# Vision tower block with routed experts: the residual travels halved with each fetched row

## The chip, the cores and the metric

The kernel runs on one core of a Trainium2 chip. The core has five engines that run their own instruction streams and meet only at semaphores: TensorE (PE, matmul; its weight loads are listed as PEld), VectorE (DVE), ScalarE (ACT), GpSimd (POOL) and SyncE (SP, which here only issues transfers). Sixteen DMA engines move data between HBM and the on-chip memory (SBUF). The metric is the device time of one execution in microseconds (us); less is better.

## The reference, cut to what matters

```python
h = tok(x, W)                                  # 64 images x 36 patches, 192 channels: 2304 tokens
h = h + attn(layernorm(h), W_attn, b_attn, W_o, b_o)      # 12 heads, causal
flat = layernorm(h).reshape(-1, 192)
probs = softmax(flat @ router_w.T)             # 8 experts
top_w, top_i = top_k(probs, 2); top_w = top_w / top_w.sum(-1)
out = 0
for e in range(8):
    w_e = sum(top_w * (top_i == e))
    out = out + w_e * (gelu(flat @ w1[e] + b1[e]) @ w2[e] + b2[e])   # 192 -> 768 -> 192
return h + out                                 # layernorm: (x - mean) / sqrt(var + 1e-5)
```

## The kernel before

Tokens are worked on in 22 tiles (`NT`) of 108 rows (`TT`, three images); the last tile has only 36 real rows (`LAST`). Every product is made of fp16 high and low parts, three matmuls for one.

**Embedding and attention.** `embed` and `h_out` (ACT) fill `H`, the residual of all 22 tiles side by side in SBUF (108 x 22*192 fp32). A software pipeline over steps `i` then runs attention for tile `i`, and `residual(i - 2)` (DVE, L694) adds the projected output to `H`. `stats2` and the norm2 functions make the second layer norm of the tile from `H`; its high and low halves go to the row buffer `RB` (in `REG`), 194 fp32 words a token: 192 words of normed data (`rows2`) and two words `GAP` and `SECOND` for the gate weights.

**Routing.** After the last tile DVE chooses two experts for each token, and counts, ranks and places the 4608 (token, expert) pairs in a table of 43 tiles (`NS`) of 128 rows, each tile of one expert. `SOURCE` says which token each of the 128 rows of a tile reads, `TARGET` to which row of `yrows` its result goes (spare rows past the end for empty places). Meanwhile SP, once the gates are made (`route` at `GATES`) and the normed rows are done (`n2_lo`), stores `RB` to `xrows` in HBM in one transfer (L363).

**Experts.** For each of the 43 tiles `s`: POOL gathers 128 rows of `xrows` into a ring of four buffers `XR` (`gather_rows`, L435); PE transposes them (`transpose_rows`, L1107); DVE copies the transposes to `YT` and makes the gate of each row (`rows_out`, L870 and L873); PE multiplies by W1 (`up`, L1140); ACT does gelu and its fp16 high half (`hidden`, L596 and L601), DVE the low half (`hidden_lo`, L610); PE multiplies by W2 (`down`, L1156, the bias at L1161); DVE scales the PSUM result by the gate into `YO` (`gated`, L885); POOL scatters `YO` to `yrows` (`store_rows`, L440). Order by hand: POOL issues gathers 0 to 5, then for each `s` store `s` and gather `s + 6`. PE's iteration `s` holds `up(s + 2)`, `transpose_rows(s + 4)`, `down(s)`. A gather waits until its ring buffer was transposed (`xr_mm`) and its gate read (`gate_done`).

**Last pass.** The two results of a token lie side by side in `yrows`. In five batches (`BATCHES`, of 6, 6, 6, 3 and 1 token tiles) SP loads both parts (L368), DVE adds the first part to `H` and then the second (L907), and SP stores the batch to `out` (L371). All five loads are issued before the first store, on the one queue of SP.

Of the kernel before, what the change touches and what calls it, by code (L numbers as in the profile page):

```python
# [26 lines left out]
TT = TI * T  # L27
# [16 lines left out]
TOPK = 2  # L44
ST_ = 128
NS = TOPK * B * T // ST_ + E - 1
GAP, SECOND, ROW = C, C + 1, C + 2
SPARE = NS * ST_
CODED = 2048 // TT
CODES = 2 * TOPK  # L50
# [1 line left out]
S_X, S_W = 2.0 ** 8, 2.0 ** 10  # L52
S_XW = S_X * S_W
S_Q, S_V, S_P, S_G = 2.0 ** 6, 2.0 ** 8, 2.0 ** 12, 2.0 ** 6
EPS = 1e-5
PRODUCTS = [(0, 0), (0, 1), (1, 0)]
LAST_COLUMN = 2 * 127
LOADED = 8
# [8 lines left out]
def build(nc, xt, wtok, wqkv, wo, wr, w1, w2, idf, idh, selq, causal, kmask, eid,  # L67
# [3 lines left out]
    with ctx:  # L71
# [30 lines left out]
        WSTG = sb("WSTG", [128, WSLOTS * F])  # L102

        XW = KT * TT
        REG = sb("REG", [128, max(6 * XW, NT * ROW)])
        XHL = REG[:, 4 * XW:6 * XW].bitcast(F16)
        XS = [REG[:, n * XW:(n + 1) * XW] for n in range(4)]
        XS += [W1R[1][:, 2 * (E * F - n * XW):2 * (E * F - (n - 1) * XW)].bitcast(F32) for n in range(XSLOTS - 4, 0, -1)]
        RB = REG[0:TT, 0:NT * ROW]
        RBH = RB.bitcast(F16)  # L110

        KROW = 2 * 2 * 2 * TT
# [35 lines left out]
        G = PTR[:, 0:2 * F]  # L148
        GP = [PTR[:, (2 + p) * F:(3 + p) * F].bitcast(F16) for p in range(2)]

        XRS = 4
        XR = [REG[:, 6 * 2 * C + n * ROW:6 * 2 * C + (n + 1) * ROW] for n in range(XRS)]

        BATCHES, at = [], 0
        for tiles, home in ((6, REG[0:TT, 0:6 * 2 * C]), (6, W2[0][0:TT, 0:6 * 4 * C].bitcast(F32)),
# [112 lines left out]
            return buf[:, t % 2 * cols:(t % 2 + 1) * cols]  # L268

        def rows2(t, at, cols):  # L270
            return RBH[:, t * 2 * ROW + at:t * 2 * ROW + at + cols]

        PIECES = 2 * E
        PROJ, ROUT = 208, 448
# [9 lines left out]
            return range(max(0, 3 * i // 2), min(2 * PIECES, 3 * (i + 1) // 2))  # L284

        FIRST_NORM, GROUP, DRAIN = 8, 4, 3
        EMBEDDED = {11: -6, 13: -5, 15: -4, 17: -3, 19: -2, 21: -1}

        def has(t):
# [23 lines left out]
        @block.sync  # L313
        def _(sp):
            def patches(t):
                sp.dma_start(XS[t % XSLOTS], xt[t]).then_inc(x_in[t % XSLOTS], 16)

            def values_in(t):
                need(sp, vl_done, t + 2)
                need(sp, o_mm, t - 2)  # L320
                ring = t % VRING
                for b in range(TI):
                    for h in range(GH):
                        src = VP[b * T:(b + 1) * T, :].rearrange("p (t h r) -> p t h r", t=VRING, h=GH)[:, ring:ring + 2, h, :]
                        dst = VB[h * T:(h + 1) * T, :].rearrange("p (t b h r) -> p t b h r", t=VRING, b=TI, h=GH)[:, ring:ring + 2, b, h, :]
                        sp.dma_start(dst, src).then_inc(v_in[t // 2 % 2], 16)

            def weights(n):
                need(sp, w_lo, n - WSLOTS + 1)
                slot = n % WSLOTS * F  # L330
                at = n % PIECES
                if n < PIECES:
                    sp.dma_start(WSTG[0:HCP, slot:slot + F], w1[:, at * F:(at + 1) * F]).then_inc(w_in[n % WSLOTS], 16)
                else:
                    half = W2E // 2
                    sp.dma_start(WSTG[:, slot:slot + half], w2[:, at * half:(at + 1) * half]).then_inc(w_in[n % WSLOTS], 16)

            sp.dma_start(LANDED[0], wtok).then_inc(raw_in[0], 16)
            for t in range(XSLOTS):
                patches(t)  # L340
            for n in range(1, len(SMALL)):
                sp.dma_start(LANDED[n], SMALL[n][0]).then_inc(raw_in[n], 16)
            for dst, src in CONSTS:
                sp.dma_start(dst[:, :], src).then_inc(const_in, 16)
            for t in range(XSLOTS, NT):
                sp.wait_ge(xl_done, t - XSLOTS + 1)
                patches(t)
            for n in range(WSLOTS):
                weights(n)
            sp.wait_ge(consts_set, FILLS)  # L350
            for i in range(-2, NT + 1):
                for n in pieces(i - 1):
                    if n + WSLOTS < 2 * PIECES:
                        weights(n + WSLOTS)
                if has(i + 2) and i % 2 == 0:
                    values_in(i + 2)

            sp.wait_ge(s_mm, NT)
            for dst, src in LATER:
                sp.dma_start(dst, src).then_inc(later_in, 16)  # L360
            sp.wait_ge(n2_lo, NT)
            sp.wait_ge(route, GATES)
            sp.dma_start(xrows.rearrange("(t p) c -> p t c", p=TT), RB.rearrange("p (t c) -> p t c", c=ROW)).then_inc(rows_stored, 16)  # L363
            for u in range(2):
                sp.wait_ge(y_stored[u], 16 * ((NS + 1 - u) // 2))
            for n, (t, tiles, home) in enumerate(BATCHES):
                rows = yrows[t * TT * TOPK:(t + tiles) * TT * TOPK, :].rearrange("(t p k) c -> p t (k c)", t=tiles, k=TOPK)
                sp.dma_start(home.rearrange("p (t c) -> p t c", t=tiles), rows[0:home.shape[0]]).then_inc(parts_in[n], 16)  # L368
            for n, (t, tiles, home) in enumerate(BATCHES):
                sp.wait_ge(summed, 2 * n + 2)  # L370
                sp.dma_start(out[t * TT:min((t + tiles) * TT, B * T), :].rearrange("(t p) c -> p t c", t=tiles),  # L371
                             H[0:home.shape[0], t * C:(t + tiles) * C].rearrange("p (t c) -> p t c", c=C)).then_inc(out_stored, 16)
            sp.wait_ge(out_stored, 16 * len(BATCHES))
# [3 lines left out]
        def _(gp):  # L377
# [53 lines left out]

            def gather_rows(s):
                need(gp, xr_mm, s - XRS + 1)
                need(gp, gate_done, s - XRS + 1)
                gp.indirect_dma_start(out=XR[s % XRS], out_offset=None, in_=xrows,  # L435
                                      in_offset=bass.IndirectOffsetOnAxis(ap=SOURCE[:, s:s + 1], axis=0)).then_inc(rows_in[s % XRS], 16)

# [2 lines left out]
                gp.indirect_dma_start(out=yrows, out_offset=bass.IndirectOffsetOnAxis(ap=TARGET[:, s:s + 1], axis=0),  # L440
                                      in_=YO[s % 2], in_offset=None).then_inc(y_stored[s % 2], 16)

            gp.wait_ge(rows_stored, 16)
            gp.wait_ge(table, 5)
            for s in range(6):
                gather_rows(s)
# [8 lines left out]
        def _(act):  # L455
# [8 lines left out]

            def h_out(t):
                act.wait_ge(emb_mm, t + 1)
                nc.scalar.activation(htile(t), bank(5 + t % 2, TT, C), ACT.Copy, scale=1 / S_XW).then_inc(h_done, 1)

            def inverse_deviation(n):
                a, b = NORMS[n]  # L470
# [137 lines left out]
        def _(dve):  # L608
# [82 lines left out]
            def residual(t):  # L691
                need(dve, op_mm, t + 1)
                need(dve, o_mm, upto(t + 2))
                nc.vector.scalar_tensor_tensor(htile(t), bank(6, TT, 512)[:, PROJ:PROJ + C], 1 / S_XW, htile(t), ALU.mult, ALU.add).then_inc(h2_done, 1)  # L694

            def logits(t):
                need(dve, r_mm, t + 1)
# [92 lines left out]
            last = CHOSEN[:, (NT - 1) * E:NT * E]  # L790
            nc.vector.tensor_scalar(last, last, REAL[:, 0:1], None, ALU.mult).then_inc(route, 1)

            carry = RB.rearrange("p (t c) -> p t c", c=ROW)
            dve.wait_ge(gap_exp, 1)
            nc.vector.tensor_scalar(col[6], col[1], 1.0, S_G * S_W, ALU.add, ALU.mult).then_inc(route, 1)
            routed(15)
# [84 lines left out]
            def gated(s):  # L881
                dve.wait_ge(down_mm, s + 1)
                dve.wait_ge(gate_done, s + 1)
                need(dve, y_stored[s % 2], 16 * (s // 2))
                nc.vector.tensor_scalar(YO[s % 2], bank(4 + s % 2, ST_, C), GATE[:, s:s + 1], None, ALU.mult).then_inc(y_done, 1)  # L885

            rows_out(0)
            rows_out(1)
# [11 lines left out]
            for n, (t, tiles, home) in enumerate(BATCHES):  # L900
                dve.wait_ge(parts_in[n], 16)
                part = home.rearrange("p (t k c) -> p t k c", t=tiles, k=TOPK)
                for k in range(TOPK):
                    if k:
                        dve.wait_ge(summed, 2 * n + 1)
                    h = H[0:home.shape[0], t * C:(t + tiles) * C].rearrange("p (t c) -> p t c", c=C)
                    nc.vector.tensor_tensor(h, h, part[:, :, k, :], ALU.add).then_inc(summed, 1)  # L907


        @block.tensor  # L910
# [352 lines left out]
```

## Time and profile before

| | |
|---|---|
| median of 3 runs | 481.61 us (478.01 to 483.15) |
| the profiled execution | 475.52 us, of it the span from first to last instruction 473.6 us |
| PE busy | 372.1 us (79%) |
| DVE busy | 276.4 us (58%) |
| ACT busy | 221.1 us (47%) |
| POOL busy | 189.3 us (40%) |
| mean granted TensorE clock | 0.889 |

The profile is of one execution. Its stages, in us from the start of the span: embedding and attention up to about 230, routing 230 to 259, experts 259 to 450, last pass 452 to 473. Busy shares are averages over these stages, so each is looked at by itself: what a wait in one of them is worth is read from its timeline.

### The profile page before, as it was taken

To read this page: it belongs to the slowest core of one execution; us is meant where nothing else is said; L and a number is where in the kernel's file an instruction comes from. 1 tells how busy PE (TensorE), PEld (TensorE's weight loads), DVE (VectorE), ACT (ScalarE), POOL (GpSimd) and SP (SyncE) were. 2 spreads that over 40 slices of the span, in tenths; PEclk is the share of its full clock that TensorE was granted. 3 is DMA by queue.
4 is the path that set the end of the run, shared out by engine and by line. 5 is a ranking of instruction groups with operands and counts; after the bars stand their busy time and mean duration, and the time that the engine had idled before them with its cause. 6 is when DMAs were issued, how large, how long until landed. Compare 5 with 4: busy or idle time off the path is not lost.

```text
span 473.6 us, 16224 instructions
## 1 busy us (share of the span) xinstructions
PE 372.1 (79%) x6386; PEld 339.0 (72%) x6386; DVE 276.4 (58%) x739; ACT 221.1 (47%) x450; POOL 189.3 (40%) x214
## 2 busy tenths in 40 slices
PE   2687879879879897875344799998998999999900
PEld 2677768879878786764322798898998998999700
DVE  2565467985989898853598244344443444444426
ACT  3555557766879786844200233443344333444200
POOL 9016314434647462445201434344443444443300
PEclk9999988986999999965555699999999999999965
DMA  8765003333233323320050211111111111121057
GB/s 301 190 180 155 5 18 82 103 80 77 88 101 105 100 65 92 80 66 1 0 158 0 52 35 50 40 53 51 44 51 45 53 50 44 46 54 43 36 201 256
DMA packets 29047, 38.47 MB, mean 81 GB/s; under 512 B 12104, under 2 KB 20704, under 8 KB 28976
## 3 DMA queue, kind: packets, MB, share of 16 engines
q1 hardware_dynamic: 24848, 28.94, 21.0%
q0 software_dynamic: 4128, 8.50, 6.1%
q8 instruction: 55, 0.90, 0.8%
q14 instruction: 16, 0.13, 0.1%
HBM read 27.65 MB, written 7.84 MB: 75 GB/s over the span
## 4 chain that ended last, share of the span: by engine, by line
PE 43%; DVE 16%; issue 15%; POOL 11%; ACT 7%; DMA 7%; SPq 1%; POOLq 0%; DVEq 0%; ACTq 0%
PE PSA L1140 17%; PE PSA L1156 10%; PE PSA L918 3%; POOL XF L401 3%; DMA W2l<-yrows 3%; PE PSA L950 2%; DMA W2l<-wqkv 2%; DVE VB L843 2%; PE PSA L1161 2%; DVE REG L610 2%; PE PSA L1002 2%; PE PSA L1107 2%; POOL yrows L440 2%; DMA REG<-xrows,KBR 2%; POOL YP L411 2%
## 5 line engine op out<-in xcount | busy, mean ns | idle before, releaser
L1140 PE MATMUL PSA<-YT,W1h 97*128 97x128 f16 x1032 | 93.4, 222 | 5.4 <-ACT PTR L596 4.6
L596 ACT ACTIVATE PTR<-PSA 128x768 f32<-128x768 f32 x43 | 34.9, 811 | 127.6 <-PE PSA L1140 126.7
L1140 PE MATMUL PSA<-YT,W1l 97*128 97x128 f16 x516 | 90.5, 221 | 0.0
L1140 PEld LDWEIGHTS PSA<-YT,W1h 97*128 x1032 | 79.1, 99 | 12.3 <-issue 11.9
L440 POOL DMA_INDIRECT yrows<-KBR x43 | 43.1, 1002 | 93.5 <-DVE KBR L885 93.5
L1156 PE MATMUL PSA<-W2h,PTR 128*128 x516 | 71.1, 246 | 0.2 <-DVE PTR L610 0.2
L1156 PE MATMUL PSA<-W2l,PTR 128*128 x258 | 63.5, 246 | 0.0
L610 DVE SCALAR_TENSOR_TENSOR PTR<-PTR 128x768 f16<-128x768 f32 x43 | 41.2, 959 | 34.6 <-ACT PTR L601 33.1
L885 DVE TENSOR_SCALAR KBR<-PSA,KBR 128x192 f32<-128x192 f32 x43 | 18.0, 418 | 72.2 <-PE PSA L1161 70.5
L435 POOL DMA_INDIRECT REG<-xrows,KBR x43 | 42.1, 980 | 44.5 <-DVE KBR L864 31.7
L918 PE MATMUL PSA<-W2h,REG 128*108 128x192 f16 x396 | 38.1, 256 | 18.6 <-DVE REG L610 18.6
L1140 PEld LDWEIGHTS PSA<-YT,W1l 97*128 x516 | 51.2, 99 | 0.0
L918 PEld LDWEIGHTS PSA<-W2h,REG 128*108 128x108 f16 x396 | 35.2, 135 | 20.8 <-DVE REG L610 11.5
L1156 PEld LDWEIGHTS PSA<-W2h,PTR 128*128 128x128 f16 x516 | 47.2, 98 | 0.9 <-issue 0.8
L601 ACT ACTIVATE PTR<-PTR 128x768 f16<-128x768 f32 x43 | 36.3, 843 | 11.2 <-PE PSA L1161 8.9
L411 POOL TENSOR_TENSOR YP<-YF,YP 108x192 f16<-108x192 f32 x22 | 19.3, 878 | 49.1 <-ACT YP L532 49.1
L390 POOL TENSOR_SCALAR XF<-H,MEAN,RS 108x192 f32<-108x192 f32 x22 | 28.3, 1286 | 22.0 <-DVE RS L653 22.0
L950 PE MATMUL PSA<-XN,WAh 97*128 97x108 f16 x352 | 30.6, 221 | 3.4 <-issue 2.8
L401 POOL TENSOR_SCALAR XF<-H,MEAN,RS 108x192 f32<-108x192 f32 x22 | 22.1, 1008 | 20.8 <-DVE RS L653 20.8
L950 PEld LDWEIGHTS PSA<-XN,WAh 97*128 97x128 f16 x352 | 27.3, 104 | 3.8 <-issue 3.8
L950 PE MATMUL PSA<-XN,WAl 97*128 97x108 f16 x176 | 29.3, 220 | 0.0
L1002 PE MATMUL PSA<-VB,PTR 108*128 108x51 f16 x792 | 26.7, 193 | 2.7 <-DVE PTR L610 2.7
(164 smaller groups left out, 880.9 us busy)
## 6 DMA issues: line engine op xcount, KB each, us to landing
WSTG<-w SPq DMA_DIRECT2D x32, 336.0 KB, 3.3
REG<-xt SPq DMA_DIRECT2D x12, 324.0 KB, 4.7
W1l<-xt SPq DMA_DIRECT2D x10, 324.0 KB, 3.5
VB<-VP SPq DMA_DIRECT2D x99, 19.1 KB
xrows<-REG SPq DMA_DIRECT2D x1, 1800.6 KB
out<-H SPq DMA_DIRECT2D x3, 486.0 KB
REG<-yrows SPq DMA_DIRECT2D x1, 972.0 KB
W2h<-yrows SPq DMA_DIRECT2D x1, 972.0 KB
```

The source lines that it names most:

```text
L401: nc.gpsimd.tensor_scalar(two(XF[1], t, C), htile(t), MEAN[:, NT + t:NT + t + 1], RS[:, NT + t:NT + t + 1], ALU.subtract, ALU.mult).then_i ...
L411: nc.gpsimd.tensor_tensor(yp[:, C:2 * C], two(YF, t, C), yp[:, 0:C], ALU.subtract).then_inc(yl_done, 1)
L435: gp.indirect_dma_start(out=XR[s % XRS], out_offset=None, in_=xrows, in_offset=bass.IndirectOffsetOnAxis(ap=SOURCE[:, s:s + 1], axis=0)).t ...
L440: gp.indirect_dma_start(out=yrows, out_offset=bass.IndirectOffsetOnAxis(ap=TARGET[:, s:s + 1], axis=0), in_=YO[s % 2], in_offset=None).the ...
L596: nc.scalar.activation(g.rearrange("p (h c) -> p h c", h=2), PSA[:, 2 * u * 512:(2 * u + 2) * 512].rearrange("p (h c) -> p h c", h=2)[:, : ...
L601: nc.scalar.activation(GP[0][:, u * F:(u + 1) * F], g, ACT.Copy, scale=S_G).then_inc(gh_done, 1)
L610: return nc.vector.scalar_tensor_tensor(dst, src, scale, hi, ALU.mult, ALU.subtract)
L918: ins = nc.tensor.matmul(bank(5 + t % 2, TT, C), xhl(t % 2, a)[:, k * TT:(k + 1) * TT], WT[b][:, k * C:(k + 1) * C], start=n == 0, stop=n ...
L950: ins = nc.tensor.matmul(bank(0, 128, 4 * TT)[:, j * TT:(j + 1) * TT], WA[a][:, c * WQKV + j * HC:c * WQKV + j * HC + 128], xn(t, b, c), s ...
L1002: ins = nc.tensor.matmul(o, PT[p][:, at:at + 128], value_blocks(t)[:, b, :, q, g, :], start=n == 0, stop=n == 3 * TI - 1)
L1140: ins = nc.tensor.matmul(bank(2 * u + f // (FC // 2), 128, FC // 2 * ST_)[:, w:w + ST_], weights[a, c], YT[:, at:at + ST_], start=k == 0, ...
L1156: nc.tensor.matmul(bank(4 + u, ST_, C), GP[a][:, at:at + ST_], weights[b], start=(f, a, b) == (0, 0, 0), stop=False)
```

## The change

`H` is kept at half its value: `h_out` and `residual` scale by 0.5, and `EPS` becomes a quarter of what it was, which leaves the layer norm's result the same. A row of `xrows` grows from 194 to 386 words: behind the normed data and the gate words come the 192 words of the halved residual. SP stores them straight from `H`, in two transfers (tiles 0 to 17, then 18 to 21), ahead of the transfer of `RB`, which now writes rows at a pitch of 386 words. Each gather brings 386 words a row. `gated` multiplies by the gate and adds the row's halved residual in one instruction; two such rows per token make the whole residual. The ring `XR` has eight buffers (four in `REG`, four in `WSTG`), and a gather waits until `gated` is done with its buffer (`y_done`) where it waited for the gate. The last pass adds the two parts into `H`, one instruction a batch where there were two.

```diff
-GAP, SECOND, ROW = C, C + 1, C + 2
+GAP, SECOND, NORMED, ROW = C, C + 1, C + 2, 2 * C + 2
+HALF = 0.5
-EPS = 1e-5
+EPS = 1e-5 / 4
-        REG = sb("REG", [128, max(6 * XW, NT * ROW)])
+        REG = sb("REG", [128, max(6 * XW, NT * NORMED)])
-        XRS = 4
-        XR = [REG[:, 6 * 2 * C + n * ROW:6 * 2 * C + (n + 1) * ROW] for n in range(XRS)]
+        XRS = 8
+        XR = [REG[:, 6 * 2 * C + n * ROW:6 * 2 * C + (n + 1) * ROW] for n in range(XRS // 2)]
+        XR += [WSTG[:, n * ROW:(n + 1) * ROW] for n in range(XRS // 2)]
+        EARLY = 18
...
+            rows = xrows.rearrange("(t p) c -> p t c", p=TT)
+            for a, b in ((0, EARLY), (EARLY, NT)):
+                sp.wait_ge(h2_done, b)
+                sp.dma_start(rows[:, a:b, NORMED:ROW], H[:, a * C:b * C].rearrange("p (t c) -> p t c", c=C)).then_inc(rows_stored, 16)
             sp.wait_ge(n2_lo, NT)
             sp.wait_ge(route, GATES)
-            sp.dma_start(xrows.rearrange("(t p) c -> p t c", p=TT), RB.rearrange("p (t c) -> p t c", c=ROW)).then_inc(rows_stored, 16)
+            sp.dma_start(rows[:, :, 0:NORMED], RB.rearrange("p (t c) -> p t c", c=NORMED)).then_inc(rows_stored, 16)
...
-                sp.wait_ge(summed, 2 * n + 2)
+                sp.wait_ge(summed, n + 1)
...
             def gather_rows(s):
                 need(gp, xr_mm, s - XRS + 1)
-                need(gp, gate_done, s - XRS + 1)
+                need(gp, y_done, s - XRS + 1)
...
-            gp.wait_ge(rows_stored, 16)
+            gp.wait_ge(rows_stored, 16 * 3)
...
-                nc.scalar.activation(htile(t), bank(5 + t % 2, TT, C), ACT.Copy, scale=1 / S_XW).then_inc(h_done, 1)
+                nc.scalar.activation(htile(t), bank(5 + t % 2, TT, C), ACT.Copy, scale=HALF / S_XW).then_inc(h_done, 1)
...
-                nc.vector.scalar_tensor_tensor(htile(t), bank(6, TT, 512)[:, PROJ:PROJ + C], 1 / S_XW, htile(t), ALU.mult, ALU.add).then_inc(h2_done, 1)
+                nc.vector.scalar_tensor_tensor(htile(t), bank(6, TT, 512)[:, PROJ:PROJ + C], HALF / S_XW, htile(t), ALU.mult, ALU.add).then_inc(h2_done, 1)
...
-                nc.vector.tensor_scalar(YO[s % 2], bank(4 + s % 2, ST_, C), GATE[:, s:s + 1], None, ALU.mult).then_inc(y_done, 1)
+                nc.vector.scalar_tensor_tensor(YO[s % 2], bank(4 + s % 2, ST_, C), GATE[:, s:s + 1], XR[s % XRS][:, NORMED:ROW],
+                                               ALU.mult, ALU.add).then_inc(y_done, 1)
...
                 part = home.rearrange("p (t k c) -> p t k c", t=tiles, k=TOPK)
-                for k in range(TOPK):
-                    if k:
-                        dve.wait_ge(summed, 2 * n + 1)
-                    h = H[0:home.shape[0], t * C:(t + tiles) * C].rearrange("p (t c) -> p t c", c=C)
-                    nc.vector.tensor_tensor(h, h, part[:, :, k, :], ALU.add).then_inc(summed, 1)
+                h = H[0:home.shape[0], t * C:(t + tiles) * C].rearrange("p (t c) -> p t c", c=C)
+                nc.vector.tensor_tensor(h, part[:, :, 0, :], part[:, :, 1, :], ALU.add).then_inc(summed, 1)
```

In the order of SP's queue, between the small tables that routing needs (`KBR`) and the loads of the last pass, there stood before (sizes are partitions x tiles x words):

```order
L360 DMA KBR<-codes 108x44
L360 DMA KBR<-spare 128x43
L363 DMA xrows<-REG 108x22x194 [waits route,norm2_lo]
L368 DMA REG<-yrows 108x6x384 [waits y_stored1,y_stored0]
L368 DMA W2h<-yrows 108x6x384
```

and stands now:

```order
L363 DMA KBR<-codes 108x44
L363 DMA KBR<-spare 128x43
L367 DMA xrows<-H 108x18x192 [waits h2_done]
L367 DMA xrows<-H 108x4x192 [waits h2_done]
L370 DMA xrows<-REG 108x22x194 [waits route,norm2_lo]
L375 DMA REG<-yrows 108x6x384 [waits y_stored1,y_stored0]
```

The two transfers from `H` have come in ahead of the one from `REG`; nothing else on this queue has moved.

On DVE, from the last tiles of the experts to the last pass, there stood before:

```order
L610 SCALAR_TENSOR_TENSOR PTR<-PTR 128x768 [waits gh_done]
L885 TENSOR_SCALAR KBR<-PSA,KBR 128x192 [waits y_stored1,gate_done,down_mm]
L885 TENSOR_SCALAR KBR<-PSA,KBR 128x192 [waits y_stored0,gate_done,down_mm]
L907 TENSOR_TENSOR H<-H,REG 108x1152 [waits parts_in0]
L907 TENSOR_TENSOR H<-H,REG 108x1152 [waits summed]
L907 TENSOR_TENSOR H<-H,W2h 108x1152 [waits parts_in1]
L907 TENSOR_TENSOR H<-H,W2h 108x1152 [waits summed]
```

and stands now:

```order
L617 SCALAR_TENSOR_TENSOR PTR<-PTR 128x768 [waits gh_done]
L892 SCALAR_TENSOR_TENSOR KBR<-PSA,KBR,REG 128x192 [waits y_stored1,gate_done,down_mm]
L892 SCALAR_TENSOR_TENSOR KBR<-PSA,KBR,REG 128x192 [waits y_stored0,gate_done,down_mm]
L912 TENSOR_TENSOR H<-REG 108x1152 [waits parts_in0]
L912 TENSOR_TENSOR H<-W2h 108x1152 [waits parts_in1]
L912 TENSOR_TENSOR H<-W2l 108x1152 [waits parts_in2]
```

The gated row reads one more operand, with the same waits; five additions of the last pass are gone, with their waits, and none has changed its place.

## Rows read from the trace of the kernel before

**Rows 1.** The page: 40 slices of the span, PE busy and granted PE clock.

```profile
PE   2687879879879897875344799998998999999900
...
PEclk9999988986999999965555699999999999999965
```

**Rows 2.** Waits of PE, 273 to 450 us: us in total, times, longest.

```profile
PE PSA L1140 <- ACT PTR L596: 4.6, 4, 1.2
PE PSA L1107 <- DMA REG<-xrows,KBR: 0.6, 1, 0.6
```

**Rows 3.** SP's timeline, 200 to 300 us: start, duration, what.

```profile
206.28 0.36 SPq L360 DMA_DIRECT2D KBR<-spare  x1
236.03 0.32 SPq L363 DMA_DIRECT2D xrows<-REG  x1
```

**Rows 4.** Windows: PE, PEld, DVE, ACT, POOL busy, PE clock, DMA share, GB/s.

```profile
207.00:214.00 7.00, 4.75 (x58) 4.33 (x56) 4.27 (x18) 2.90 (x9) 2.90 (x4) 0.50 0.03 4
214.00:220.00 6.00, 4.14 (x30) 3.37 (x30) 2.01 (x8) 3.15 (x8) 3.75 (x7) 0.50 0.01 3
```

**Rows 5.** Windows around the store of the rows, and around one gather.

```profile
240.00:242.00 2.00, 0.48 (x3) 0.25 (x3) 1.87 (x11) 0.00 (x0) 0.00 (x0) 0.50 0.84 234
...
369.40:370.80 1.40, 1.40 (x21) 1.08 (x19) 0.42 (x1) 1.01 (x2) 0.00 (x0) 1.00 0.29 71
```

**Rows 6.** POOL's timeline, 255 to 330 us; in brackets the idle time before.

```profile
259.26 1.19 POOL L435 DMA_INDIRECT REG<-xrows,KBR  x1 [31.66 <-DVE KBR L864]
260.76 0.96 POOL L435 DMA_INDIRECT REG<-xrows,KBR  x1 [0.30 <-issue]
...
278.90 0.98 POOL L435 DMA_INDIRECT REG<-xrows,KBR  x1 [0.31 <-issue]
...
299.40 0.97 POOL L435 DMA_INDIRECT REG<-xrows,KBR  x1 [0.30 <-issue]
```

**Rows 7.** Chain that ended last, in order of time: two waits for fetched rows.

```profile
260.76 2.61 DMA REG<-xrows,KBR
...
299.40 4.76 DMA REG<-xrows,KBR
```

**Rows 8.** PE's timeline: the transposes of tiles 6 and 11.

```profile
281.83 0.39 PE L1107 MATMUL PSA<-IDH,REG 128*96 128x128 f16 x4
...
304.20 0.42 PE L1107 MATMUL PSA<-IDH,REG 128*96 128x128 f16 x4 [0.62 <-DMA REG<-xrows,KBR]
```

**Rows 9.** Lines: duration ns min/median/max, first and last start, shapes.

```profile
L885 DVE TENSOR_SCALAR KBR<-PSA,KBR x43: 417/418/419, 275.8 to 449.1; 128x192 f32<-128x192 f32 x43
...
L694 DVE SCALAR_TENSOR_TENSOR H<-PSA,H x22: 347/358/358, 77.6 to 220.0; 108x192 f32<-108x192 f32 x22
...
L435 POOL DMA_INDIRECT REG<-xrows,KBR x43: 945/973/1191, 259.3 to 430.8; - x43
```

**Rows 10.** DVE's timeline, 446 to 474 us: the additions of the last pass.

```profile
458.68 2.75 DVE L907 TENSOR_TENSOR H<-H,REG 108x1152 f32<-108x1152 f32 x2 [9.16 <-DMA REG<-yrows]
...
465.28 2.75 DVE L907 TENSOR_TENSOR H<-H,W2l 108x1152 f32<-108x1152 f32 x2 [0.55 <-DMA W2l<-yrows]
...
469.42 0.73 DVE L907 TENSOR_TENSOR H<-H,W2l 36x192 f32<-36x192 f32 x2
```

**Rows 11.** SP's timeline, 446 to 474 us: last load, and the five stores.

```profile
457.55 1.28 SPq L368 DMA_DIRECT2D W2l<-yrows  x1
461.46 9.02 SPq L371 DMA_DIRECT2D out<-H  x5
```

**Rows 12.** Windows of the last pass, columns as in rows 4.

```profile
460.60:463.90 3.30, 0.00 (x0) 0.00 (x0) 2.71 (x3) 0.00 (x0) 0.00 (x0) 0.50 0.80 299
...
466.00:469.00 3.00, 0.00 (x0) 0.00 (x0) 2.93 (x4) 0.00 (x0) 0.00 (x0) 0.50 0.82 279
469.00:472.40 3.40, 0.00 (x0) 0.00 (x0) 1.11 (x3) 0.00 (x0) 0.00 (x0) 0.50 0.80 270
```

**Rows 13.** DMA of 465.6 to 473.6 us: packets and their sizes.

```profile
DMA packets 2461, 1.88 MB, mean 235 GB/s; under 512 B 83, under 2 KB 2461, under 8 KB 2461
```

More of the change, by code:

```diff
@@ L108, in build @@
         XS += [W1R[1][:, 2 * (E * F - n * XW):2 * (E * F - (n - 1) * XW)].bitcast(F32) for n in range(XSLOTS - 4, 0, -1)]
-        RB = REG[0:TT, 0:NT * ROW]
+        RB = REG[0:TT, 0:NT * NORMED]
         RBH = RB.bitcast(F16)
@@ L270, in rows2 @@
         def rows2(t, at, cols):
-            return RBH[:, t * 2 * ROW + at:t * 2 * ROW + at + cols]
+            return RBH[:, t * 2 * NORMED + at:t * 2 * NORMED + at + cols]
         PIECES = 2 * E
@@ L791, in _ @@
             nc.vector.tensor_scalar(last, last, REAL[:, 0:1], None, ALU.mult).then_inc(route, 1)
-            carry = RB.rearrange("p (t c) -> p t c", c=ROW)
+            carry = RB.rearrange("p (t c) -> p t c", c=NORMED)
             dve.wait_ge(gap_exp, 1)
```

## The prediction

> **What bounds the kernel now.** I read the page's slices first, to cut the span into stages [rows 1]. The reader is to see that PE is nearly full from 273 us to 450, at the full clock, and nearly idle in the two stages around it: routing (230 to 259) and the last pass (after 452). So a saving on DVE counts only in those two, and in the experts' stage only what PE waits for counts.
>
> The waits of PE over 273 to 450 say how much that is [rows 2]: 4.6 us behind gelu's line, and one wait of 0.6 us for fetched rows. In the experts' stage DVE, ACT and POOL all wait for PE. The transfers that the change touches have 0.6 us of the path there, but they are the ones that could take more of it.
>
> Then the last pass, in four views. DVE's timeline shows ten additions in pairs, the pairs of the three large batches 2.75 us each [rows 10]. A look at that alone makes DVE seem the bound from 465.28 us on, since from there it works without a gap until 469.42 + 0.73 = 470.15. The windows say otherwise: the DMA share is 0.80 to 0.82 at 299 GB/s before 464 us and 279 and 270 GB/s after it, flat to 472.4 us [rows 12]. And the packet sizes say what moves: from 465.6 us on there are 1.88 MB in 2461 packets, 0.76 KB each [rows 13]. A load row is 1536 B, a store row 768 B, and the five stores are 2304 rows, 1.77 MB. So nearly all of the stores' bytes move after 465.6 us, although SP issued the first at 461.46 [rows 11]: stores stand behind all the loads on SP's queue. The other 0.11 MB of the 1.88 are the end of the loads, 0.4 us, so the loads end at 466.0. From there 1.77 MB at 279 GB/s are 6.3 us, to 472.3. The last pass is one unbroken stream of transfers, and DVE works in its shadow.
>
> **Part 1: five additions less in the last pass.** DVE loses half of its work there: 2.75 / 2 = 1.37 us for each of three batches, and half of the 2.1 us from 468.0 to 470.15 for the two small ones, 5.2 us in all. What does it free? A store has to be in the queue before the queue comes to it. With the loads done at 466.0 and 0.498 MB (1.78 us) for each of the large stores, the third is wanted at 469.6 us, the fourth at 471.4, the last at 472.2. Before, the third was issued after 465.28 + 2.75 = 468.0, the fourth at 469.5 and the last at 470.15: each was in time by 1.6 us or more. Coming earlier brings nothing. I take 0. The cover is the backlog of stores; if it were gone, and the end hung on DVE, the additions from 465.28 to 470.15 (4.87 us) would halve: 2.4 us gained. That is the lower bound of this part.
>
> **Part 2: the halved residual is stored.** 22 x 108 rows of 768 B are 1.82 MB more. The store of the normed rows, with 776 B a row, ran at 234 GB/s [rows 5], so the two new transfers take 6.4 and 1.4 us. SP reaches them at 206.6, behind the small tables [rows 3]; tile 17 is done by then, so the first runs from 207 to 214, and the second follows the last residual (220.0 + 0.4 [rows 9]) and ends near 223. The DMA share in that time is 0.03 and 0.01 [rows 4], and SP has nothing else until 236.03. So neither is on the path, and the old transfer is issued when it was. Its 1.84 MB are 7.9 us at 234 GB/s, so it ends near 245, and the first gather starts at 259.26 [rows 6]: 14 us of cover for the threefold wait. Its rows now lie 1544 B apart, in the same number and size of pieces: 0. What could leak is that the steps of attention in 207 to 214 share memory with a busy queue. No row shows such a price; the nearest is the store of rows during routing, beside which DVE was busy 1.87 us of 2.00 [rows 5], so not held up. 0, at most 1 us.
>
> **Part 3: gathers of 386 words.** One gather is 128 rows, eight for each of 16 engines. In the window 369.4 to 370.8 exactly one (99 KB) moved: 0.29 x 1.4 us x 16 / 128 = 51 ns of an engine a row. The bulk rows give the price of length: 17.4 GB/s an engine for 776 B (234 / (0.84 x 16)) is 45 ns a row [rows 5], 23.4 GB/s for 1536 B (299 / (0.80 x 16)) is 66 ns [rows 12]. So twice the length costs 21 ns a row by bulk, 51 if the gather's row simply doubles: 8 rows an engine, 0.17 to 0.41 us later. I take 0.25, nearer the bulk rows, which show that much of a row's time doesn't grow with it.
>
> By the Trainium skill (DMA: Bandwidth & Descriptors, section "Anatomy of one DMA — SWDGE (gpsimd) path") such a DMA takes 2.0 us and its bytes at 436 GB/s; for 99 KB that is 2.2 us and for 198 KB 2.5, an estimate of 0.23 us more, and the sum by it would be the same to 0.1 us. This trace has 2.61 us for one with 99 KB [rows 7].
>
> Where does 0.25 us show? The rows of tile 1 start at 260.76 and land 2.61 us later, with PE waiting: on the path, +0.25 (tile 0, issued earlier, is covered by it). Gather 6 starts at 278.90 and is wanted at 281.83 [rows 6, 8]: 2.93 us for 2.61, so 0.3 us of cover, 0 to +0.1. Gather 11 starts at 299.40, and PE stands idle 0.62 us for it until 304.20 [rows 7, 8]: +0.25. From it I read the rhythm: wanted 4.80 - 0.62 = 4.18 us after its start, so the usual gather, at 2.6 us, has 1.57 us of cover. The other 30 or so cost 0, unless one is as late as gather 11 was. Sum 0.5 us, bounds 0.3 and 1.0.
>
> **Part 4: the ring.** Gather `s + 6` now waits for `y_done` of tile `s - 2`, but POOL has already waited for that of tile `s` at the store ahead of it: 0. Gathers 4 and 5 no longer wait for the first transposes, but POOL was issuing at its own pace (0.30 us between [rows 6]), and they are wanted 10 us later: 0.
>
> **Part 5: the gated row.** A fifth operand. The tensor-scalar takes 418 ns; the nearest row to the new form, the residual's line, also PSUM and SBUF in and 192 wide, takes 358 with a constant instead of a scalar from memory [rows 9]. So between 358 and, say, the two together less nothing shared, 776; I take 418. It stands on the path once, for the last tile (bound: +0.36); in all others POOL's store and gather move with it, inside the 1.57 us. All scale constants: 0.
>
> **Sum.** 475.52 us for the profiled execution, + 0.5 = 476.0. That execution is 6.1 us under the median of the three runs, so on the median: 481.61 + 0.5 = 482.1. About 1% (4.8 us) is what a measurement of this kernel can tell from no change.
>
> **Rivals.**
> *The last pass hangs on DVE after all.* For it: DVE is busy without a gap to 470.15, and the chain of waits runs through it. Against: a flat rate and packets of store size only. It would give -2.4 + 0.5: 479.7, still within 1%.
>
> *POOL makes the gather's descriptors by bytes, not by rows.* The price: the instruction goes from 0.97 to 1.94 us, so a gather lands 0.97 + 0.41 = 1.38 us later. It is under the 1.57 us of cover, so most tiles don't notice, but tile 1 pays it and the longer issue of tile 0 ahead of it (0.97 + 1.38 = 2.35), gather 6 1.38 - 0.32 = 1.1, gather 11 1.38, and one more straggler about 0.5: +5.3 us, 486.9. It decides from 1.57 us on: an excess then comes back every second tile (gather, transpose and store form a loop over two), about 18 times; 0.5 us of excess would be 9 us. For it: no row here shows two sizes of gather. Against: a gather and a scatter of 128 rows take about the same, and PE's own wait is only 0.6. The Trainium skill's same section calls descriptor generation small in its cost; no run here shows it for longer rows.
>
> *Gathers disturbed oftener.* Gather 11 took 4.76 us where others take 2.6, with one row size smaller. If longer rows double such events, each costs 0.5 to 1 us: +2 to 3 us, 484.
>
> **Chances.** Forecast (-1 to +2 us) 0.68; last pass on DVE 0.10; more stragglers 0.10; gather by bytes 0.09; something else 0.03. Faster by over 1% needs both a gain that I don't see and luck in the median: 0.05. Slower by over 1%: the case by bytes, half of it just over the line, and part of the stragglers: 0.13. Within 1%: 0.82. Range: down to 479.7 for the DVE case less 1.7 for a median of three that spread over 5 us, 478; up to 487 for the case by bytes.
>
> **What would show it.** The first transposes after 262 us later by 0.2 to 0.4. Gathers on POOL still at 0.97 us (at 1.9 the rival is true). PE's wait for fetched rows about 1 us in 273 to 450. In the last pass, DVE idle between single additions, stores issued from 460 us, and the same flat 280 GB/s; from the end of the last gated row (449.5) to the end of the span the same 24.1 us. Wrong would be: 22 us there, PE waits for rows in every second tile, or a gated row over 0.8 us.

## The result, and the profile after

The changed kernel takes 480.82 us (median of 20 runs), the kernel before 479.03 us in as many runs beside it. The ratio is 1.0075, with a 95% interval of 1.0039 to 1.0111: 3.6 us slower (1.9 to 5.3). The medians are over all runs and differ by 1.8 us, while the ratio, here and below, takes of each kernel only the runs within 1.5% of its own fastest (475.82 us for the changed kernel, 472.49 for the kernel before), which are 16 of 20 and 11 of 20. So 3.6 us is the larger of two readings; where it matters below, both are given. The profiled execution has a span of 478.2 us against 473.6.

To see where the time went I cut each profiled execution at three instants: start of the first gather on POOL, start of the first gated row on DVE, start of the last gated row. (A gated row is the DVE instruction that multiplies a tile's result by its gate; the last column runs from the start of the last one to the end of the span.) In us, from the timelines of POOL and DVE:

| | first gather starts | to first gated row | first to last gated row | last gated row to end |
|---|---|---|---|---|
| before | 259.26 | 16.56 | 173.29 | 24.49 |
| changed | 259.80 | 17.07 | 177.04 | 24.29 |
| difference | +0.54 | +0.51 | +3.75 | -0.20 |

The experiments below are divided in the same way. In e1_long_only, e9_tail128_split8 and e11_tail128 the profiled execution is a long one (483.5, 480.6 and 484.1 us), but its first gather starts only at 265.70, 271.85 and 272.86 us, so the excess lies ahead of the stages that are read.

**The last pass** is as it was, by DVE's timeline and the windows of the changed kernel (the columns of rows 10 and 12):

```profile
463.24 1.36 DVE L912 TENSOR_TENSOR H<-REG 108x1152 f32<-108x1152 f32 x1 [8.91 <-DMA REG<-yrows]
466.48 1.36 DVE L912 TENSOR_TENSOR H<-W2h 108x1152 f32<-108x1152 f32 x1 [1.88 <-DMA W2h<-yrows]
469.72 1.36 DVE L912 TENSOR_TENSOR H<-W2l 108x1152 f32<-108x1152 f32 x1 [1.88 <-DMA W2l<-yrows]
```

```profile
465.00:468.00 3.00, 0.00 (x0) 0.00 (x0) 1.36 (x1) 0.00 (x0) 0.00 (x0) 0.50 0.80 301
468.00:471.00 3.00, 0.00 (x0) 0.00 (x0) 1.28 (x1) 0.00 (x0) 0.00 (x0) 0.50 0.80 294
471.00:474.00 3.00, 0.00 (x0) 0.00 (x0) 1.10 (x3) 0.00 (x0) 0.00 (x0) 0.50 0.82 279
```

DVE's idle gaps between batches grew from 0.55 us [rows 10] to 1.88, by about what the additions lost (2.75 less 1.36), and the transfers run at the same share and rate as before [rows 12].

**The gathers.** The chain of waits of the changed kernel has the rows of tile 1 landing after 3.01 us, where it was 2.61 [rows 7]:

```profile
261.29 3.01 DMA REG<-xrows,KBR
264.43 0.66 PE PSA L1112 x4
```

and the waits of PE over 273 to 455 us now hold two for fetched rows (the first is shown without its releaser, but stands before the transposes too, L1112; the second is for a buffer of `WSTG`), where they held one of 0.6 [rows 2]:

```profile
PE PSA L1145 <- ACT PTR L603: 5.2, 5, 1.4
PE PSA L1112 <- issue: 1.0, 1, 1.0
PE PSA L1112 <- DMA WSTG<-xrows,KBR: 0.8, 1, 0.8
```

The instructions themselves cost what they did. By line (ns min/median/max), a gather is 0.06 us longer on POOL than in rows 9, and the gated row, now with five operands, takes the same 418 ns:

```profile
L442 POOL DMA_INDIRECT REG<-xrows,KBR x23: 946/1032/1187, 259.8 to 435.3; - x23
...
L892 DVE SCALAR_TENSOR_TENSOR KBR<-PSA,KBR,REG x23: 417/418/419, 276.9 to 453.9; 128x192 f32<-128x192 f32 x23
```

**Tile by tile.** The starts of the 43 gated rows are 4.09 us apart in both kernels but for a few; the time of tile `s` is from the gated row of `s - 1` to its own. PE transposes the rows of gather `s + 4` just ahead of `down(s)`, so a gather that lands late shows at the tile four before it: gather 6 at tile 2, gather 11 at tile 7, gather 31 at tile 27, gather 41 at tile 37. Tiles 5, 13, 21 and 29 are about 1.1 us longer in either kernel, and the ones where the kernels differ by more than 0.05 us account for 3.7 of the 3.75 us:

| tile | 2 | 7 | 21 | 27 | 37 |
|---|---|---|---|---|---|
| before | 4.10 | 4.91 | 5.34 | 4.09 | 4.31 |
| changed | 4.38 | 5.25 | 7.14 | 5.07 | 4.59 |

Tile 21 is something else than the rest. PE's only wait over 355 to 372 us is one of 1.4 us for ACT; there is none for rows. By the windows of the changed kernel its granted clock was down:

```profile
362.60:365.00 2.40, 1.10 (x20) 1.13 (x21) 1.59 (x3) 1.15 (x2) 1.41 (x2) 1.00 0.22 88
365.00:367.00 2.00, 2.00 (x26) 1.99 (x24) 0.23 (x2) 0.44 (x1) 0.62 (x1) 0.61 0.35 88
367.00:369.80 2.80, 2.80 (x23) 2.39 (x22) 0.07 (x1) 0.38 (x2) 0.00 (x0) 0.67 0.07 22
```

Between 365.0 and 369.8 us it stood for some 3.4 us at the lower of its two levels, 1.2 GHz (an estimate from the means 0.61 and 0.67), after a stretch in which PE had been busy 1.10 us of 2.40. Work at half the clock for 3.4 us loses 1.7 us; the tile took 1.80 us longer than before. PE stands idle for 1.1 to 1.4 us ahead of the same line at about this place in the other kernels too, and their clock stays up, so the wait alone doesn't bring the dip.

**The stores of the residual** are hidden. SP began with the tables at 204.86, had issued both residual transfers by 221.2, and issued the old transfer at 236.56:

```profile
204.86 0.33 SPq L363 DMA_DIRECT2D KBR<-real  x1
...
207.29 13.93 SPq L367 DMA_DIRECT2D xrows<-H  x2
236.56 0.29 SPq L370 DMA_DIRECT2D xrows<-REG  x1
```

From tables to the old transfer it is 31.70 us, 31.79 before [rows 3: 236.03 less 204.24, the start of the same row in the timeline of before].

### The profile page after: what moved, and what is told of

Same layout as the page of the kernel before. It is cut to its first block, busy times and chain, and to the rows that moved or that the text cites. A ratio compares the mean times of both kernels' runs of the same rounds, so it can differ in the third digit from the quotient of the medians.

```text
span 478.2 us, 16217 instructions
## 1 busy us (share of the span) xinstructions
PE 377.1 (79%) x6386; PEld 343.0 (72%) x6386; DVE 271.2 (57%) x734; ACT 221.2 (46%) x450; POOL 190.7 (40%) x214
## 4 chain that ended last, share of the span: by engine, by line
PE 41%; DVE 14%; issue 12%; ACT 9%; POOL 8%; DMA 7%; another core or an unknown queue 6%; SPq 1%; DVEq 0%; POOLq 0%; ACTq 0%
PE PSA L1145 15%; PE PSA L1161 9%; PE PSA L923 3%; PE PSA L955 3%; DMA W2h<-yrows 3%; POOL XF L408 3%; ACT PTR L603 2%; DVE VB L850 2%; DMA W2l<-wqkv 2%; DVE REG L617 2%; PE PSA L1007 2%; PE PSA L1166 2%; POOL YP L418 2%; DVE PTR L849 1%
## 5 line engine op out<-in xcount | busy, mean ns | idle before, releaser
L1161 PE MATMUL PSA<-W2h,PTR 128*128 x516 | 72.1, 248 | 0.2 <-DVE PTR L617 0.2
L442 POOL DMA_INDIRECT REG<-xrows,KBR x23 | 23.5, 1021 | 38.4 <-DVE KBR L871 31.7
L955 PE MATMUL PSA<-XN,WAh 97*128 97x108 f16 x352 | 31.9, 226 | 3.4 <-issue 2.8
L955 PEld LDWEIGHTS PSA<-XN,WAh 97*128 97x128 f16 x352 | 28.3, 107 | 3.8 <-issue 3.8
L955 PE MATMUL PSA<-XN,WAl 97*128 97x108 f16 x176 | 30.6, 225 | 0.0
L892 DVE SCALAR_TENSOR_TENSOR KBR<-PSA,KBR,WSTG 128x192 f32<-128x192 f32 x20 | 8.4, 418 | 39.0 <-PE PSA L1166 39.0
L892 DVE SCALAR_TENSOR_TENSOR KBR<-PSA,KBR,REG 128x192 f32<-128x192 f32 x23 | 9.6, 418 | 35.6 <-PE PSA L1166 33.9
```

The lines of the kernel that those rows point to most:

```text
L955: ins = nc.tensor.matmul(bank(0, 128, 4 * TT)[:, j * TT:(j + 1) * TT], WA[a][:, c * WQKV + j * HC:c * WQKV + j * HC + 128], xn(t, b, c), s ...
L1161: nc.tensor.matmul(bank(4 + u, ST_, C), GP[a][:, at:at + ST_], weights[b], start=(f, a, b) == (0, 0, 0), stop=False)
```

## The experiments

**Theory A:** the longer gathers cost the time, by landing later, at the start of the stage and at a few tiles whose rows already came late. **Theory B:** they don't; the profiled 4.6 us are the chance of one execution (the clock at tile 21, a later start). A third matter is the last pass: what bounds it, and whether the change opens something there.

### The long gathers alone

The kernel before, with

```diff
-GAP, SECOND, ROW = C, C + 1, C + 2
+GAP, SECOND, NORMED, ROW = C, C + 1, C + 2, 2 * C + 2
...
+            sp.dma_start(rows[:, :, NORMED:ROW], H[:, :].rearrange("p (t c) -> p t c", c=C)).then_inc(rows_stored, 16)
+            sp.dma_start(rows[:, :, 0:NORMED], RB.rearrange("p (t c) -> p t c", c=NORMED)).then_inc(rows_stored, 16)
```

> The kernel before, with rows of 386 words in xrows and fetched whole (the residual is stored behind the normed rows and not used; ring of four, two additions a batch as before). Theory A, the longer gathers cost the time: from the start of the first gather to the first gated row 17.0 to 17.2 us (before 16.56, changed kernel 17.07), from the first to the last gated row 174.5 to 176 us (before 173.3, changed kernel 177.0 with a dip of the clock in it), ratio to before 1.003 to 1.007. Theory B, the chance of the one profile (a dip of the clock at tile 21, a later start): ratio 1.000, and the first gated row as before.

Measured: ratio 1.0022 (0.9982 to 1.0061). To the first gated row 17.51 us, a little over what A expects: over the 9.3 to 14.3 us after the first gather TensorE's granted clock was 0.75 on average, where it was 0.91 in the changed kernel over 9.2 to 14.2. First to last 174.97 us, tile 21 in 5.57, tiles 2, 7, 27 and 37 in 4.26, 5.30, 4.72 and 4.58. The experts' stage is as A says, with neither the ring nor the fifth operand of the gated row nor the new last pass. The ratio's interval holds B's 1.000 and most of A's range (1.003 to 1.007), so it decides nothing.

### The change without long gathers

The changed kernel with rows of 194 words; the halved residual goes to a buffer of its own and is not added.

```diff
-GAP, SECOND, NORMED, ROW = C, C + 1, C + 2, 2 * C + 2
+GAP, SECOND, NORMED, ROW = C, C + 1, C + 2, C + 2
...
-                sp.dma_start(rows[:, a:b, NORMED:ROW], H[
+                sp.dma_start(xhalf.rearrange("(t p) c -> p t c", p=TT)[:, a:b, :], H[
...
+                nc.vector.tensor_scalar(YO[s % 2], bank(4 + s % 2, ST_, C), GATE[:, s:s + 1], None, ALU.mult).then_inc(y_done, 1)
```

> The changed kernel with short gathers: 194 words a row, the halved residual stored to a buffer of its own and not added (this part of the result is left out); ring of eight, wait on y_done, one addition a batch stay. Theory A: first gather to first gated row 16.6 us, first to last gated row 173.3 us or 0.3 less, tail 23.9 us, ratio to before 0.999 to 1.001. Theory B or a cost in the other parts (the stores during attention, the ring): ratio as the changed kernel's, 1.004 to 1.011.

Measured: ratio 1.0016 (0.9987 to 1.0046). To the first gated row 16.83, first to last 173.63 us, tiles 7, 27 and 37 in 4.88, 4.54 and 4.37, tile 2 in the usual time. So by the stages the stores during attention, the ring and the wait on `y_done` cost nothing that shows; what does comes with the longer row. The ratio alone can't tell, since its interval overlaps with the changed kernel's (1.0039 to 1.0111). The last pass of this one execution took 27.08 us, 2.8 more than in the changed kernel with the same code: the transfers kept the same share (0.79 to 0.81 from 458 to 473 us) but moved 262 to 289 GB/s instead of 278 to 301, and DVE waited 3.12 and 2.53 us between the large batches instead of 1.88. Why they were slower isn't known.

### One addition alone

The kernel before with one addition a batch, of the two parts only; the residual is left out.

```diff
-                for k in range(TOPK):
...
+                h = H[0:home.shape[0], t * C:(t + tiles) * C].rearrange("p (t c) -> p t c", c=C)
+                nc.vector.tensor_tensor(h, part[:, :, 0, :], part[:, :, 1, :], ALU.add).then_inc(summed, 1)
```

> The kernel before with one addition a batch, of the two parts only (the residual is left out of the result). If the last pass is bound by its transfers, as predicted: last gated row to the end 23.9 to 24.1 us (before 24.07), ratio 1.000. If DVE bounds it: 21.7 us, ratio 0.995.

Measured: ratio 1.0011 (0.9975 to 1.0048). Last gated row to end 24.60 us, counted from its start as in the table above (24.49 before). Halving DVE's work in the last pass gains nothing that shows (had DVE been the bound, 2.4 us were expected): it is bound by its transfers. The experts' stage took 173.65 us here, so with short rows and six ahead it is 173.3 to 173.65 in three executions.

### Gathers eight ahead

The changed kernel with

```diff
-            for s in range(6):
+            for s in range(8):
                 gather_rows(s)
...
-                if s + 6 < NS:
-                    gather_rows(s + 6)
+                if s + 8 < NS:
+                    gather_rows(s + 8)
```

> The changed kernel with gathers eight tiles ahead of the stores instead of six (the ring of eight allows it). Theory A with late rows as the mechanism: PE's waits for fetched rows after the first tiles fall from 1.8 us to 0, tiles 2, 7 and 27 come in the usual 4.09 us, first to last gated row 173 to 173.5 us plus any dip of the clock, ratio to before 1.000 to 1.003 with only the first rows still 0.4 us later. If the longer rows cost through something else than their landing (contention, the stores), ratio stays at 1.004 to 1.011.

Measured: ratio 0.9979 (0.9939 to 1.0020). First to last gated row 172.15 us; tiles 2, 7, 27 and 37 in 4.09, and PE's waits over 273 to 455 us hold none for rows:

```profile
PE PSA L1145 <- issue: 4.5, 4, 1.2
PE PSA L1161 <- DVE PTR L617: 0.2, 1, 0.2
```

So the late landings are the mechanism in this stage: the same long rows, asked for two tiles sooner, cost nothing here, and the stage is faster than before. A cost of the long rows by another way than their landing would have stayed.

The same with short rows, the kernel before with a ring of eight:

> The kernel before with a ring of eight short rows and gathers eight ahead; residual and last pass as before. Theory A: tiles 7, 27 and 37 lose their 0.8, 0.5 and 0.3 us, first to last gated row 172.1 us (before 173.3 and 173.65), ratio to before 0.995 to 0.999, so the gain of eight ahead is nearly the same with short rows and with long ones. If instead the 172.15 us of the long-row kernel with eight ahead was luck: 173.3 us.

Measured: first to last gated row 172.19 us, as A says, but ratio 1.0083 (1.0036 to 1.0130), against the expectation. By the medians of all runs (481.26 and 480.57 us) the difference is 0.7 us. Something is lost all the same, since the gain of the stage doesn't arrive, and the way to the first gated row shows where: 18.64 us instead of 16.56. ACT's first gelu was late. By ACT's timeline of this kernel:

```profile
276.05 0.81 ACT L596 ACTIVATE PTR<-PSA 128x768 f32<-128x768 f32 x1 [34.76 <-remote]
```

though the last matmul of the product that it needs had ended 2.1 us before, at 273.94. Of the three executions with eight gathers at once, this and that of e5 had the late start (18.64 and 18.69 us), that of e4 had not (16.87). In both, long rows or short, the first gelu starts 11.4 us after the first gather; in e4 it is 9.6. The late start costs 2.1 us and the stage gives back 1.1, so the stages say +1.0 us: near the medians' 0.7, and short of the ratio's 4.0.

### The longer row again

> The changed kernel with rows of 570 words (184 words of the residual stored once more behind it, fetched and not used), gathers six ahead. Theory A, dose and effect: each gather lands another 0.3 to 0.5 us later; first gather to first gated row 17.4 to 17.7 us, tiles 2, 7, 27 and 37 each 0.3 to 0.5 us longer than in the changed kernel, first to last gated row 176 to 178 us, ratio to before 1.008 to 1.016. If bytes are not the cause: as the changed kernel, 175.2 us and 1.004 to 1.008.

The edit, on the changed kernel: `ROW` is 570, and two more transfers on SP store 184 words of the residual at `HALVED:ROW`.

Measured: ratio 1.0144 (1.0076 to 1.0211). To the first gated row 17.64 us, as expected: 16.6, 17.1, 17.6 for 194, 386 and 570 words, about 0.5 us a step. The rows of tile 1 land after 3.81 us (2.61 and 3.01 with 194 and 386 words). Tile 2 took 4.66 us (4.10, 4.3 to 4.4, 4.66). But tiles 7 and 27 took the usual time, tiles 36 and 37 took 4.58 and 4.66, and the stage 174.31 us, less than with 386 words, where 176 to 178 was expected. So the expectation missed for the stage: stragglers didn't grow by bytes, and which tiles are hit depends on something that moved; what it is stays open. The ratio is in the range, but it stands for 6.9 us (3.6 to 10.1), and the stages explain 2 (1.1 at the start, 1.0 in the experts). The medians of all runs (6 and 23) differ by 3.1 us.

### The changed kernel once more

> The changed kernel as it is, once more. If the long tile 21 (7.14 us, at a granted clock of 0.61 to 0.67) was one execution's chance: tile 21 takes 5.3 us, first to last gated row 175.2 us, tiles 2, 7, 27 and 37 long again (4.4, 5.3, 4.7 to 5.1 and 4.6 us); ratio 1.004 to 1.008. If the change itself brings the dip: tile 21 at 7 us again.

Measured: ratio 1.0065 (1.0016 to 1.0113); the medians of all runs differ by 0.8 us. To the first gated row 17.06 us, first to last 174.91, tile 21 in 5.31, tiles 2, 7 and 27 in 4.32, 5.16 and 4.78, tile 36 and 37 in 4.33 and 4.61. The dip of the clock was one execution's chance; none of the other 13 profiled executions has it. The long tiles come back at the same places. With long rows and six ahead the stage took 174.6 to 175.0 us in three executions, and 177.04 - 1.80 = 175.24 in the first.

### The last pass on 128 partitions

With `H` no longer an operand, the last pass needn't keep the tiles of 108 rows. The changed kernel with eight ahead and

```diff
+            parts = yrows[0:TOPK * B * T, :].rearrange("(p n) c -> p (n c)", p=128)
+            for n, (t, tiles, home, _) in enumerate(BATCHES):
+                sp.dma_start(home, parts[:, t * TOPK * C:(t + tiles) * TOPK * C]).then_inc(parts_in[n], 16)
+            sums = out.rearrange("(p n) c -> p (n c)", p=128)
...
+        for tiles in (6, 6, 4, 2):
```

> The changed kernel with gathers eight ahead and a last pass on 128 partitions: since H is no longer an operand, partition p takes tokens 18p to 18p + 17, in four batches of 6, 6, 4 and 2 tokens a partition; loads are rows of up to 9.2 KB, stores up to 4.6 KB. If the last pass is bound by transfers that keep only 0.80 of the sixteen engines busy: 299 / 0.80 = 374 GB/s at a share of 1, 5.31 MB take 14.2 us where they took 18.4, last gated row to the end of the span about 20 to 20.5 us (24.3 to 25 before), ratio to before 0.988 to 0.992. If it is bound by HBM or by DVE: 24 us as before, ratio 0.998.

Measured: ratio 0.9885 (0.9791 to 0.9980). Last gated row to end 19.42 us, first to last 172.15. By its windows the transfers now fill the engines' time:

```profile
457.00:460.00 3.00, 0.00 (x0) 0.00 (x0) 1.23 (x1) 0.00 (x0) 0.00 (x0) 0.50 1.02 433
460.00:463.00 3.00, 0.00 (x0) 0.00 (x0) 1.49 (x2) 0.00 (x0) 0.00 (x0) 0.50 0.98 382
463.00:466.00 3.00, 0.00 (x0) 0.00 (x0) 1.51 (x2) 0.00 (x0) 0.00 (x0) 0.50 0.98 346
```

share 0.98 to 1.02 instead of 0.80, and 346 to 433 GB/s instead of 270 to 301. Several things changed together: the number of partitions, the length of a row (up to 9.2 KB for 1536 B) and the number of batches, four for five; no run here separates them. The Trainium skill (DMA: Bandwidth & Descriptors, section "Why a DMA increments its semaphore by 16 and not by 1") says that a transfer is split over the largest number of engines up to 16 that divides the slowest dimension of both its sides, which is 12 for 108 and 16 for 128. By that 108 partitions could keep 12/16 = 0.75 of the engines; the measured 0.80 is above it, and 0.80 to 0.98 or 1.02 is 0.82 or 0.78, so the trace points that way without confirming the count of engines.

The same without the gathers ahead, so the changed kernel plus this last pass alone:

> The changed kernel with nothing but the last pass on 128 partitions, gathers six ahead: tail 19.4 us (24.3), first to last gated row 174.9 to 175.3 us with tiles 2, 7, 27 and 37 long again, ratio to before 0.994 to 0.998.

Measured: ratio 0.9893 (0.9836 to 0.9950), better than expected; last pass 19.45 us, first to last gated row 174.62 us, tiles 2, 27 and 37 in 4.37, 4.79 and 4.40 and tile 7 in 4.68. Without eight gathers at once the first gated row comes after 17.17 us, where e5 had 18.69.

### Six gathers at once, two later

To keep eight ahead without eight in a row, in the changed kernel with eight ahead:

```diff
+                if s == 6:
+                    gp.wait_ge(gh_done, 1)
                 gather_rows(s)
```

> The changed kernel with those gathers, the last pass as it was changed. Gathers late by theory A: first to last gated row 172.2 us, ratio to before 0.996 to 1.000. If the 0.998 of the run with eight ahead was one chip's chance (its twin with short rows gave 1.008 though its experts took 172.19 us): 1.003 to 1.008.

Measured: ratio 0.9970 (0.9935 to 1.0005). To the first gated row 17.21 us, first to last 172.11, last pass 24.26. POOL's and ACT's timelines show gathers 6 and 7 behind the first gelu's high half, and ACT released in the usual way:

```profile
269.66 1.54 POOL L442 DMA_INDIRECT WSTG<-xrows,KBR  x1 [4.30 <-ACT PTR L610]
271.51 0.95 POOL L442 DMA_INDIRECT WSTG<-xrows,KBR  x1 [0.31 <-issue]
```

```profile
267.71 0.81 ACT L605 ACTIVATE PTR<-PSA 128x768 f32<-128x768 f32 x1 [33.17 <-PE PSA L1147]
```

The same on the kernel before, with short rows:

> The kernel before with a ring of eight short rows, six gathers at once and two after the first gelu. First gather to first gated row 16.5 us, first to last 172.2 us, ratio to before 0.996 to 0.999. If eight ahead costs something outside the experts' stage: 1.003 or more again, as in the run with eight at once (1.008).

Measured: ratio 0.9964 (0.9927 to 1.0002), to the first gated row 16.54 us, first to last 172.15. It doesn't have the 1.008 of its twin with eight at once.

And all together, long rows, the last pass on 128 partitions, gathers six and two:

> The last pass on 128 partitions and gathers eight ahead, of which the first six start at once and the seventh and eighth only after the first gelu's high half is made. If eight gathers in a row are what made ACT start 1.7 us late in two of three profiles: first gather to first gated row 16.9 to 17.1 us, first to last 172.2 us, tail 19.4 us, ratio to before 0.983 to 0.988. If the late start has another cause it comes back here (18.6 us) and the ratio stays near 0.9885.

Measured: 471.37 us against 478.91, ratio 0.9824 (0.9775 to 0.9873), a little better than expected: 17.07, 172.18 and 19.50 us by stage. It is faster than both kernels. Against the kernel before the stages say 1.1 us in the experts and 5.0 in the last pass, less 0.5 at the start, 5.6 in all; the ratio stands for 8.4 us (6.1 to 10.8) and the medians differ by 7.5, so 2 to 3 us lie outside the stages read here. In three executions out of three with the split the first gated row was in time, in two of three with eight at once it wasn't; that is in favour of the crowd of gathers as the cause, but six executions are no proof, and what ACT waited for isn't known.

## Why the prediction was right or wrong, point by point

The forecast was 482.1 us in a range of 478 to 487, +0.5 us on the kernel before. The time of 480.82 lies inside, but the kernel before came out at 479.03, and the difference is +3.6 us (1.9 to 5.3) by the ratio and +1.8 by the medians, within 1% and on the side of slower. That the time itself lies only 1.3 us from the forecast is luck: the base of three runs was 2.6 us too high, and the change cost more than the +0.5 put on it. The term that fell short is that of the gathers.

**Part 1, the additions: right.** 0 was taken, 0.2 us was measured in the first pair. Over all profiled executions the last pass on 108 partitions took 24.5 to 25.3 us with two additions (four kernels) and 23.9 to 25.4 with one (six, apart from the 27.08 of e2); no difference beyond the scatter of some 1.5 us. The fall-back price of -2.4 us did not come. The view that decided it was the sizes of packets [rows 13].

**Part 2, the residual's stores: right.** Covered; the time between the two SP rows around them didn't change. Where the first gather starts varies from execution to execution, 255.8 to 262.5 us in seven executions with these stores and 259.3 to 264.7 in four without (leaving e1, e9 and e11 aside), more than all that this change does, so a price of some tenths there would not show.

**Part 3, the gathers: right in kind, short in size.** The sum had 0.25 us for a row's later landing and let it count twice. What the runs showed:
- The landing is 0.40 us later (3.01 for 2.61; 2.93 to 3.13 for 2.56 to 2.66 over the other kernels), the upper bound of the estimate. The way to the first gated row grew by 0.5 in the pair and by 0.4 to 0.5 over all (16.87 to 17.21 for 16.54 to 16.83, without e1 and the two late starts), where 0.25 stood. So the gather's own row (51 ns doubled) gave the right size for 386 words and the bulk rows did not; choosing the bulk row was the mistake. It is no law for longer rows: with 570 words the landing grows by another 0.8 us, where the same working gives 0.4. The formula of the Trainium skill quoted there, 0.23 us more, is also short of the 0.40 of this trace.
- Gather 6 had 0.3 us of cover and was given 0 to 0.1; tile 2 grew by 0.2 to 0.3 (4.26 to 4.38 for 4.10).
- "The other 30 or so cost 0, unless one is as late as gather 11 was" hid the larger term. The one profile had one straggler of 0.6 us, and I counted one. With short rows other executions have three (tiles 7, 27 and 37 in e2 and e3), and with long rows tile 2 joins them. The late ones also come later: tile 27 takes 4.72 to 5.07 us with long rows and 4.09 to 4.58 with short ones. In the experts' stage this is 174.6 to 175.2 us against 173.3 to 173.65: +1.4. Why a gather is late at all isn't known.

Together +1.9 us: the lower end of the ratio's interval, and what the medians of all runs say (+1.8). In e6, e7 and e8 too the ratio stands above the medians' difference (4.0 for 0.7, 6.9 for 3.1 and 3.1 for 0.8 us), and in the first two the stages (1.0 and 2.1) lie nearer to the medians. So much of what the stages don't show is probably the way the ratio picks its runs; no run here settles it.

The rival with "gathers disturbed oftener" (+2 to 3 us) was thus nearer to what came than the forecast's own sum. The rival by which POOL makes descriptors by bytes is refuted: 1.03 us for 0.97.

**Part 4, the ring: right** that it costs nothing (e2, 173.63 us for the stage); it was seen only as a price. That it permits eight ahead (a gather `s + 8` needs the buffer of tile `s`, whose gated row POOL has just waited for) is worth 3 us against the changed kernel's stage, and this the prediction didn't look for.

**Part 5, the gated row: right**, 418 ns with five operands.

## What to carry to other kernels

Before costing an edit at an engine, ask whether the transfers beside it leave a gap: an unbroken share of DMA time and the size of the packets showed that ten additions or five make no difference. When a fetch grows longer, a row of its own kind is a better price to scale than the bulk transfers' (0.41 us from the one, 0.17 from the other, 0.40 measured), and the cover of *every* fetch counts, with the late ones of several executions, since one profile shows only its own stragglers. An operand that is moved off the last pass can be worth nothing by itself and still free the layout: here 128 partitions with longer rows instead of 108 gave 5 us, and fetching two tiles further ahead another 1 to 3.

## What the runs showed of the hardware that was not expected

- Transfers of 108 partitions in rows of 1536 and 768 B keep a share of 0.80 to 0.82 of the DMA engines' time and 270 to 301 GB/s (262 to 289 in e2); with 128 partitions and rows of 3.1 to 9.2 KB, in the windows of e5, the share is 0.98 to 1.02 and the rate 346 to 433 GB/s.
- A gather of 128 rows costs POOL 0.97 us with rows of 776 B and 1.03 with 1544 B; it lands 2.6 us after its issue with the one and 3.0 with the other.
- A late gather has its last bytes trickling in long after the bulk. By the DMA view of the changed kernel around gather 31 (388.8 to 393.2 us, 40 slices of 0.11 us), nearly all has moved by 390.8, and single packets follow until 392.4; one packet of instructions is in that stretch:

```profile
DMA  0000000009393586910000002000200009741000
...
q8 instruction: 1, 0.02, 1.2%
```

  Gathers 11 and 31 have such a packet in the 3.2 us after their issue in the kernel before and in e8 alike. Many other gathers have one too and are in time, so it may be needed for the delay but isn't enough; which engine it holds up wasn't tried.
- A dip of TensorE's granted clock to 0.61 and 0.67 in the midst of the experts' stage cost 1.8 us in one of fourteen profiled executions; the same kernel was free of it in another (e8).
